# Reordering the expert stage of a two-layer adaLN network: last routing part ahead of the early blocks, late table in two halves

## The reference, cut to what matters

```python
flat = x.reshape(-1, D)
logits = flat @ Wr
top_vals, top_idx = jax.lax.top_k(logits, TOP_K)
weights = jax.nn.softmax(top_vals, axis=-1)
top1 = top_idx[:, 0]
w_top1 = weights[:, 0]
h = jax.nn.gelu(jnp.einsum('td,edh->teh', flat, W1), approximate=False)
y = jnp.einsum('teh,ehd->ted', h, W2)
y_sel = jnp.take_along_axis(y, top1[:, None, None], axis=1)[:, 0, :]
out = (w_top1[:, None] * y_sel).reshape(B, S, D)
```

## Time and profile before

| | us |
|---|---|
| median of 3 runs | 541.97 (540.9 to 545.82) |
| the profiled execution | 539.82 |
| its span, first to last instruction | 538.0 |
| PE / DVE / ACT / POOL busy in the span | 450.8 / 396.4 / 281.1 / 236.1 |
| routing of the last part and the 23 blocks | from about 450 to 524 of the span |
| behind the last block: store, load, gate, store | from about 524 to 538 |

### The profile page before, as it was taken

How to read it: one execution, slowest core, us unless ns; L and a number is a source line. 1 busy time by engine, 2 the same in 40 slices (tenths; PEclk the granted TensorE clock), 3 DMA queues, 4 the chain that set the end, 5 groups by cost and what they waited for, 6 DMA issues and landing times.

```text
span 538.0 us, 10393 instructions
## 1 busy us (share of the span) xinstructions
PE 450.8 (84%) x3156; PEld 272.8 (51%) x3156; DVE 396.4 (74%) x1322; ACT 281.1 (52%) x525; POOL 236.1 (44%) x334
## 2 busy tenths in 40 slices
PE   3689658897799899989997899999999997488990
PEld 3646446676674344434432444544545454387990
DVE  4689656889856588868899689889799826455544
ACT  1656797665245444453542468768678664122330
POOL 4220016999730178766753124215147346122660
PEclk9978789999989999989998699999999979789996
DMA  8990000000000533165572002313436201113115
GB/s 349 365 388 25 1 0 2 2 1 1 1 8 1 129 106 93 51 166 161 164 194 40 3 3 62 92 32 93 120 114 215 83 12 40 37 30 92 52 45 166
DMA packets 31470, 47.58 MB, mean 88 GB/s; under 512 B 3708, under 2 KB 21436, under 8 KB 30508
## 3 DMA queue, kind: packets, MB, share of 16 engines
q1 hardware_dynamic: 29448, 43.99, 26.8%
q0 software_dynamic: 1248, 2.59, 1.5%
q10 hardware_dynamic: 720, 0.34, 0.3%
HBM read 27.59 MB, written 19.12 MB: 87 GB/s over the span
## 4 chain that ended last, share of the span: by engine, by line
PE 49%; DVE 20%; issue 10%; ACT 7%; POOL 6%; DMA 5%; SPq 3%; DVEq 0%; POOLq 0%; ACTq 0%
PE ps L1954 6%; DVE arena L1308 4%; PE ps L1890 3%; PE ps L1838 3%; PE ps L2060 3%; PE ps L1892 3%; PE ps L1827 3%; PE ps L1862 3%; PE ps L1940 3%; PE ps L1665 3%; PE ps L2069 2%; DVE st L475 2%; PE ps L1753 2%; DMA arena<-expert_weights 2%; PE ps L1935 1%
## 5 line engine op out<-in xcount | busy, mean ns | idle before, releaser
L1308 DVE CUSTOM_DVE_ANT_0 arena<-ps,const 128x512 bf16<-128x512 f32 (+3 forms) x256 | 110.7, 485 | 6.9 <-PE ps L1862 6.3
L862 ACT ACTIVATE arena<-ps 128x256 f32<-128x256 f32 (+3 forms) x128 | 85.2, 703 | 37.6 <-PE ps L1940 37.0
L592 POOL TENSOR_TENSOR arena<-arena 128x512 f32<-128x512 f32 x32 | 45.7, 1427 | 59.5 <-DVE arena L1277 59.4
L1862 PE MATMUL ps<-arena 48*128 48x128 bf16 (+3 forms) x256 | 51.6, 310 | 8.4 <-DVE arena L1308 6.2
L1954 PE MATMUL ps<-arena 128*32 128x512 f32 (+3 forms) x512 | 50.9, 462 | 0.4 <-ACT arena L862 0.4
L1940 PE MATMUL ps<-arena 51*128 51x128 bf16 (+3 forms) x256 | 48.8, 309 | 0.0
L1935 PE MATMUL ps<-bconst 64*128 64x64 bf16 x512 | 42.9, 195 | 1.5 <-DMA arena<-arena 1.3
L1862 PEld LDWEIGHTS ps<-arena 48*128 48x128 bf16 x256 | 17.1, 95 | 53.0 <-DVE arena L1308 30.7
L889 ACT ACTIVATE arena<-arena 128x512 f32<-128x512 f32 x32 | 20.1, 629 | 42.4 <-DVE arena L1277 41.7
L1890 PE MATMUL ps<-arena,moe 128*128 128x512 f32 x64 | 34.9, 627 | 5.5 <-DVE arena L1260 5.4
L1088 DVE SCALAR_TENSOR_TENSOR arena<-ps,mixw,arena 128x511 f32<-128x511 f32 (+2 forms) x48 | 33.1, 738 | 6.1 <-ACT arena L740 6.1
(11 more groups left out here) (268 smaller groups left out, 1077.6 us busy)
## 6 DMA issues: line engine op xcount, KB each, us to landing
slots_x<-arena SPq DMA_DIRECT2D x1, 8910.0 KB, 39.3
arena<-expert_weights SPq DMA_DIRECT2D x32, 256.0 KB, 3.9
qk_parts<-arena SPq DMA_DIRECT2D x48, 128.0 KB, 2.4
arena<-qk_parts SPq DMA_DIRECT2D x52, 96.0 KB, 2.3
arena<-moe_in SPq DMA_DIRECT2D x4, 1025.0 KB, 5.0
moe<-moe_in SPq DMA_DIRECT2D x1, 1936.0 KB, 14.1
arena<-slots_x SPq DMA_DIRECT2D x18, 66.0 KB, 1.8
arena<-qk_parts SPq DMA_DIRECT2D x4, 288.0 KB, 5.7
```

Source lines behind the costliest of these rows:

```text
L592: pool.tensor_tensor(yacc[:, ts], yacc[:, ts], pr[:, i % 2, :], ALU.add).then_inc(sem("yacc"), 1)
L862: act.activation(pt[:, u % 4, :, 0:n], ps[:, 4 + 2 * k:6 + 2 * k, 0:n], ACT.Exp, scale=ATT_SCALE).then_inc(sem("probs"), 1)
L1308: v.tensor_tensor_reduce(out=junk[:, done % 2, 0:n], in0=ps[:, k, col:col + n], in1=w["mask"][:, (3 - qt) * P:4 * P], scale=1.0, scalar=3 ...
L1862: mm = pe.matmul(ps[:, k, col:col + n], qaug[lo:lo + KR, b % 2, 2 * g + j // 2, qt * P:(qt + 1) * P], kaug[lo:lo + KR, b % 2, 2 * g + j // ...
```

## The change

PE does `logits(2)` and `ranks(2)` ahead of the first early block, and the second `keep_busy` is gone. DVE does `positions(2)` ahead of the early blocks too; `early_table` is cut into the table and `early_taken`, which stands behind the last `o_norm`; `block_table` is cut into `blocks_left` and the rest, with block steps between; `second_best` and `top_weight` move back. POOL does the last `ln_rstd` ahead of the store of tile 11, and stores the early blocks' results between every two late blocks from the sixth on instead of every three from the seventh on. The early loads are two groups (blocks 0 and 1, and 2 to 4). On ACT `attention_T` goes ahead of `top_exp(1)`.

```diff
--- before.py
+++ after.py
@@ -248,7 +248,7 @@
         block = ctx.enter_context(nc.Block())

         PARTS_AFTER = {18: ((0, 0),), 20: ((0, 1),), 21: ((0, 2),), 28: ((1, 0),), 30: ((1, 1),), 31: ((1, 2),)}
-        GROUP_ENDS = (EARLY, 6, 8, 11, 16, NBLK)
+        GROUP_ENDS = (2, EARLY, 6, 8, 11, 16, NBLK)
         LOADED_BY_ACT = (6, 8, 10, 12, 14)
         GROUP_OF = {j: c for c, end in enumerate(GROUP_ENDS) for j in range(GROUP_ENDS[c - 1] if c else 0, end)}

@@ -660,11 +660,10 @@

             STORES_AFTER = {0: ("probs", 8 * NT - 8), 2: ("probs", 8 * NT - 5), 4: ("probs", 8 * NT - 2), 6: ("ot", NT)}

-            def to_slots(a):
-
-                lo, hi = PARTS[a]
+            def to_slots(a, lo, hi):
+
                 pool.wait_ge(sem("posu"), a + 1)
-                pool.wait_ge(sem("h4"), hi // TPB)
+                pool.wait_ge(sem("h4"), PARTS[a][1] // TPB)
                 if a == 0:
                     pool.wait_ge(sem("slots_clear"), 16)
                 for t in range(lo, hi):
@@ -683,14 +682,15 @@
                     ap=token_at[:, j:j + 1], axis=0), in_=xb[:, j, 0:D], in_offset=None)\
                     .then_inc(sem("returned"), 16)

-            to_slots(0)
-            to_slots(1)
+            to_slots(0, *PARTS[0])
+            to_slots(1, PARTS[1][0], PARTS[1][1] - 1)
             ln_rstd(pool, 4, B - 1)
-            to_slots(2)
+            to_slots(1, PARTS[1][1] - 1, PARTS[1][1])
+            to_slots(2, *PARTS[2])
             for j in range(EARLY, NBLK):
                 to_tokens(j)
-                if j >= 7 and (j - 7) % 3 == 0 and (j - 7) // 3 < EARLY:
-                    to_tokens((j - 7) // 3)
+                if j >= 6 and j % 2 == 0 and (j - 6) // 2 < EARLY:
+                    to_tokens((j - 6) // 2)


         @block.scalar
@@ -962,8 +962,8 @@
                         top_exp(0)

             weighted(NT - 1)
+            attention_T(B - 1)
             top_exp(1)
-            attention_T(B - 1)
             h4_T(3)
             for n in range(EARLY):
                 gelu(n)
@@ -1423,7 +1423,7 @@

             def early_table():

-                F, CUM, VAL, TAKEN_UPTO, TAKEN, NEXT = range(6)
+                F, CUM, VAL = range(3)
                 e = slice(0, E1)
                 b5 = blk[:, 0:EARLY, :]
                 rstep(v.scalar_tensor_tensor(out=full[:, :, :], in0=start[:, 2, :].unsqueeze(2).to_broadcast([P, E1, NT]),
@@ -1443,6 +1443,10 @@
                                        in1=blk1[:, 1, 0:EARLY, 0], op0=ALU.mult, op1=ALU.add)\
                     .then_inc(sem("expert_at"), 1)

+            def early_taken():
+
+                F, CUM, VAL, TAKEN_UPTO, TAKEN, NEXT = range(6)
+                e = slice(0, E1)
                 v.tensor_copy(early[:, TAKEN_UPTO, 0:1], w["segment8"][:, 0:1])
                 v.tensor_copy(early[:, TAKEN, E1:E1 + 1], w["segment8"][:, 0:1])
                 rstep(v.tensor_scalar(early[:, TAKEN_UPTO, 1:E1 + 1], early[:, CUM, e], float(EARLY), None, ALU.min))
@@ -1452,11 +1456,9 @@
                 rstep(v.tensor_scalar(row0[:, :], w["block"][:, 0:NBLK - EARLY], early[:, TAKEN, 0:1], float(P),
                                       ALU.add, ALU.mult))

-            def block_table():
+            def blocks_left():

                 VAL, TAKEN, NEXT = 2, 4, 5
-                rest = NBLK - EARLY
-                b18 = blk[:, 0:rest, :]
                 rstep(v.tensor_tensor(full[:, :, :], start[:, len(PARTS), :].unsqueeze(2).to_broadcast([P, E1, NT]),
                                       w["full"].rearrange("p (e t) -> p e t", e=E1), ALU.is_gt))
                 rstep(v.tensor_reduce(nblk[:, 0, :].unsqueeze(2), full[:, :, :], AX_X, ALU.add))
@@ -1464,6 +1466,12 @@
                 rstep(v.tensor_tensor_scan(nblk[:, 1, :], ones[:, 0:E1], nblk[:, 2, :], 0.0, ALU.mult, ALU.add))
                 v.scalar_tensor_tensor(out=early[:, VAL, 0:E1], in0=nblk[:, 0, :], scalar=-float(P),
                                        in1=early[:, NEXT, 0:E1], op0=ALU.mult, op1=ALU.add)
+
+            def block_table():
+
+                VAL = 2
+                rest = NBLK - EARLY
+                b18 = blk[:, 0:rest, :]
                 rstep(v.tensor_tensor(b18, nblk[:, 1, :].unsqueeze(1).to_broadcast([P, rest, E1]),
                                       w["block"][:, 0:rest].unsqueeze(2).to_broadcast([P, rest, E1]), ALU.is_le))
                 rstep(v.tensor_reduce(blk1[:, 0, EARLY:NBLK], b18, AX_X, ALU.add))
@@ -1517,7 +1525,6 @@
                     elif (it, i) == (15, 7):
                         positions(1)
                         early_table()
-                        second_best(1)

             def weights_in(n):
                 if n >= 2:
@@ -1556,43 +1563,47 @@
                     block_tokens(GROUP_OF[i])

             o_norm(NT - 1)
-            top_weight(0)
+            second_best(1)
+            early_taken()
             weights_in(0)
             attn_out(B - 1)
             router_input(B - 1, 0)
             router_input(B - 1, 1)
             weights_in(1)
+            top_weight(0)
+            top_weight(1)
             router_input(B - 1, 2)
             router_input(B - 1, 3)
             router_input(B - 1, 4)
-            top_weight(1)
+            logits_in(2)
+            choose(2)
+            positions(2)
             block_in(0)
             block_in(1)
-            logits_in(2)
-            choose(2)
+            blocks_left()
             weights_in(2)
-            positions(2)
             block_in(2)
+            block_table()
             block_out(0)
             weights_in(3)
             block_in(3)
             block_out(1)
-            block_table()
+            second_best(2)
             weights_in(4)
             block_in(4)
+            block_tokens(0)
             block_out(2)
-            second_best(2)
-            block_tokens(0)
-            v.wait_ge(sem("wtop"), 2)
+            block_tokens(1)
+            weights_in(5)
             block_out(3)
             block_out(4)
-            weights_in(5)
+            block_in(5)
+            weights_in(6)
+            block_in(6)
+            block_tokens(2)
+            v.wait_ge(sem("wtop"), 2)
             for t in range(0, 3):
                 gate_weights(t)
-            weights_in(6)
-            block_in(5)
-            block_in(6)
-            block_tokens(1)
             for i in range(6, NBLK):
                 if i < 15:
                     gate_weights(i - 3)
@@ -2078,32 +2089,29 @@
                 if i >= 1:
                     block_out(i - 1)

-            def keep_busy(n):
-                if n >= 2:
-                    pe.wait_ge(sem("h1"), DENSE + n - 1)
+            def keep_busy():
                 for _ in range(KEEP_BUSY):
-                    pe.matmul(ps[:, 4 + n % 2, 0:offsets(BPACK)[1]], identb, bconst[:, :], start=True, stop=True)
+                    pe.matmul(ps[:, 4, 0:offsets(BPACK)[1]], identb, bconst[:, :], start=True, stop=True)

             weighted_values(4 * NT - 1)
             pe.wait_ge(sem("probs"), 128)
             o_T(NT - 1)
             a_T(B - 1)
             attn_out(B - 1)
-            keep_busy(0)
+            keep_busy()
             h4_T(3)
+            logits(2)
+            ranks(2)
             ring_free(pe, 2, RING_MAIN)
             block_in(0)
             block_in(1)
-            logits(2)
             block_hidden(0)
-            ranks(2)
             block_step(1)
             block_step(2)
             block_step(3)
             block_hidden(EARLY - 1)
             block_out(EARLY - 2)
             block_out(EARLY - 1)
-            keep_busy(EARLY)
             block_in(EARLY)
             block_in(EARLY + 1)
             block_hidden(EARLY)
```

## The result

The kernel after takes 537.24 us, median of 4 runs (535.66 to 537.89); the kernel before beside it 542.65, median of 4 (540.9 to 545.82). The ratio is 0.9898, with an interval from 0.9853 to 0.9944: about 1% faster. The forecast was 537.7, in a range from 533.0 to 542.0.

What follows compares the result with a forecast made beforehand. The bound was a chain of waits across engines, no engine being full, so the first late block's start counts. 4.5 + 0.3 = 4.8 us, taken as 4.3 for the clock: 541.97 − 4.3 = 537.7, range 533.0 to 542.0.

Steps and rivals of the forecast that it cites:

- The sum of 4.3: Whole forecast gain in us: 4.5 to the first late hidden step plus 0.3 at the end, lowered for a later clock rise.
- the tail: Last token store: early results no longer stand between the late ones to the end, a gain of 0.3 us.
- Step 1: End of attention and norm: `o_norm` starts 1.0 us earlier, norm ahead of tile 11's store, `ln_apply` at 459.25, gain 1.15.
- Step 2: Last routing: logits follow the tokens at 463.6, positions come 5 us earlier, the first early hidden step stays at 469.75.
- Step 3: Early blocks with the late table cut between them: fifth hidden step at 478.45 instead of 481.01, 2.55 us earlier.
- I take the middle: Clock rise in the early blocks between 473.5 and 475.5; the later costs 1.0 of 4.8 us, so 4.3 was taken.
- Step 4: From early to late blocks without the 14 matmuls: 4.25 us between hidden steps, 1.95 of 2.65 back, first late one at 482.7.
- Step 5: End of the kernel: the last token store comes about 0.3 us behind its result, a gain of 0.3.
- Rival (a): Clock high through the last routing: chain shorter by 2.3 us, gain 7.1, time 534.9; chance 0.20.
- Rival (b): Clock low too long, PE low from 469.7 to past 487: first late hidden step at 489.3, time 543.8; chance 0.10.
- Rival (c): Routing moves, but a late load or DVE's register reads hold the fifth hidden step near 481: gain 2.25, time 539.7; chance 0.15.

## Why the forecast was right, and where not

**The time.** 537.24 against 537.7: the mechanism and the sign hold. The sum of 4.3 lies between what the pair of profiles gives (2.1) and what the medians give (5.4; by the interval 3.0 to 8.0). The pair of profiles sets an early rise of the clock (before) against a late one (after). Like with like, the fifth hidden step gains 2.5 with an early rise (28.90 behind `o_T` in before, 26.38 in after with its filler back) and 2.2 with a late one (30.12 in the second profile of before, 27.88 in after); the filler gives 1.4 and the tail 0.1, some 4 us in all, and 1 us or more on top where the fall is spared. The sum had 0.5 too much for the filler, took 0.5 off for the rise, and had no term for the fall. That the forecast came within half a us is partly luck.

**Step 1** held: `ln_apply` at 459.06 for 459.25, the norm's move 1.25 for 1.15. The early loads, which it pushes back, were covered: PE's first early transposes ran at 467.94 without a wait.

**Step 2** held within 0.35: logits 463.75 for 463.6, their read 465.64 for 465.4, `posu` 469.43 for 469.3, first hidden step 470.05 for 469.75.

**Step 3 and the clock.** The fifth hidden step came at 479.83 for 478.45. The step that failed is "I take the middle": the rise was expected between 473.5 and 475.5 and came at 475.8, just behind the late end, and the first hidden step stood 0.3 late already. Nor does the reason given for a later rise, PE's later work without a pause, show: the rise moves by some 3 us in the kernels with and without the change alike. Where it came at 473.5 in after (the filler put back), the fifth hidden step came 26.38 behind `o_T`, and 478.45 is 26.34 behind it in the profile of before: with the clock as before, the working of step 3 holds. The statement that DVE decides this step by a hair also fell: PE decided it, as the W1 copy at 479.14 shows, which waits for PE; with the clock high (pauses filled) DVE's wait was gone and the step came at 476.49.

**Step 4** had the right mechanism and the wrong size: 4.78 from the fifth to the first late hidden step for 4.25, so 1.44 of the filler's 2.65 came back and not 1.95; the filler put back cost 1.46. Load and transpose were as reckoned: ACT issued 0.95 behind the start of the fifth GELU, and PE went on 1.89 after that. Left out was the half us between that transpose and the hidden step (0.42 idle at 484.61, and 0.27 in the earlier trace rows). "Behind it PE's list, ACT's loads and the time a block are the same" does not hold in this profile: at block 8 PE waits 1.49, 0.65 more than before, and the gain falls from 2.62 to 2.00. ACT issues the load of block 10, which PE waits for there, just behind the sixth GELU in both kernels; what differs is how long it took to land. In the second profile of after the wait is 0.60. It is 0.60 to 1.49 in the six profiles with the change in which ACT has these loads, and 0.60 to 0.92 in the six without it. Whether the change makes it longer on the mean stays open.

**Step 5**: 0.14 for 0.3. The last store comes 0.47 behind its result, before 0.61.

**Rival (a)**, clock high through the routing, did not happen by itself. Its mechanism is real, as the filled pauses show, and so is its price: 2.3 off 478.45 is 24.0 behind `o_T`, and with the pauses filled the fifth hidden step came 23.9 behind it (476.49). The 4 us gained there against after hold the price and what the late rise had cost after.

**Rival (b)**, PE low past 484, did not happen in after. A clock that has risen and falls again is what happens for some us in before, in the kernel without its filler, in the one with routing ahead alone and in the one with the whole table: each time behind a wait of 2.3 to 2.9 us for the table, and in before in one profile of three. The rule of the Trainium skill, TensorE: Matmul & The Clock Gate, section "HAM oscillation — how this bites in real kernels", that waits between bursts send the clock back, agrees with those profiles, and not with the two of before in which the same wait left the clock at 1.00. In after PE is busy for 1.16 of 482 to 484 and the clock stays at 1.00, so the pause where the filler was did not do it.

**Rival (c)** was partly right: a late load holds the first late block (0.84 at 483.86) and block 8, but the fifth hidden step was not held near 481.

## What to carry to other kernels

An instruction list cut into two pieces can be worth more than its own time, where the piece in front made another engine stand still: here the table's pause in four profiles of six also cost the clock, and neither the earlier routing nor the removed filler gained anything in the kernel's time while it stood. When a filler goes, ask which wait comes next: a load that an engine issues behind its own arithmetic is late by that arithmetic. A forecast from one profile should ask whether that execution is a typical one, since two profiles of a kernel can differ by as much as the change: the clock rose up to 3 us earlier or later for the same work. A wait that is 1.49 in one profile, like that at block 8, is worth a second profile before it is explained.

## What the runs showed of the chip

A wait of PE of the same length (2.26 and 2.27 us) left the granted clock at 1.00 in two executions of before and sent it to 0.51 in a third. The rise to 1.00 in the early blocks came between 21.3 and 24.0 us behind the same point in three executions of before. Matmuls without a reader in the pauses of a latency-bound stretch kept the clock at 1.00 from 455 to 480, where it was 0.73 on the mean in after, and the fifth GELU came 4 us sooner. A load of one block that ACT issued behind the sixth GELU let PE go on 2.71 us after its issue in one execution of after and 1.83 in another. And the start of a stage moves by up to 4 us over the profiles of this study for the same work ahead of it, so profiles have to be lined up at a common point before they are subtracted.
